# Four graph layers on one core: attention's gathered rows in a ring of three buffers, its first blocks gathered under the counting stage

## The reference

```python
def _L0_gnn_ref(h, edge_index, w, fc_w, fc_b, bias):        # attention, 4 heads
    ...
    e = a_src[:, src] + a_dst[:, dst] + fc_b[0]
    e = jax.nn.leaky_relu(e, negative_slope=0.2)
    seg_max = jax.ops.segment_max(e.T, src, num_segments=n)
    e = jnp.exp(e - seg_max.T[:, src])
    ...
    agg = jax.vmap(lambda m: jax.ops.segment_sum(m, src, num_segments=n))(msg)

def spline_conv(x, row, col, basis, idx, W, b):             # layer 3, 125 kernels
    ...
    gathered = z[col[:, None] * K + idx]
    msg = jnp.einsum('es,eso->eo', basis, gathered)
    out = jax.ops.segment_sum(msg, row, num_segments=N)
    return out / jnp.maximum(deg, 1.0)[:, None] + b

h = jax.nn.elu(spline_conv(ones, row, col, basis, idx, stn1_w, stn1_b))
h = jax.nn.elu(spline_conv(h, row, col, basis, idx, stn2_w, stn2_b))
```

## Time and profile before

| | us |
|---|---|
| median of 3 runs (lowest, highest) | 6663.62 (6661.44, 6674.17) |
| the profiled execution, its time | 6661.12 |
| its span | 6659.3 |
| PE busy | 4881.0 |
| DVE busy | 4480.9 |
| POOL busy | 4088.7 |
| ACT busy | 1826.4 |

### The profile page before, as it was taken

The page is one execution under the profiler, slowest core; times in us unless marked ns, Lnnn a source line. Parts: engine busy times, 40 slices in busy tenths (PEclk is TensorE's granted clock), DMA queues, the critical chain, the costliest instruction groups (busy, mean ns, idle before and its releaser), DMA issues. The chain is left out here.

```text
span 6659.3 us, 106073 instructions
## 1 busy us (share of the span) xinstructions
PE 4881.0 (73%) x34619; PEld 3665.0 (55%) x34619; DVE 4480.9 (67%) x11674; ACT 1826.4 (27%) x3144; POOL 4088.7 (61%) x4097
## 2 busy tenths in 40 slices
PE   5444444676638888888884667999999488888885
PEld 4444444455526666666662434555555366666664
DVE  7555555469957777777771315777776687877775
ACT  1222221458824444444440000000000133333332
POOL 1777777210047777777754254777775577767773
PEclk9999999989969989999996788999999799999997
DMA  4222221123332222222226582111111211111110
GB/s 73 79 78 78 78 78 55 24 57 158 160 85 57 56 56 56 55 55 56 56 47 208 201 262 70 38 37 37 37 37 32 28 21 19 20 19 20 19 20 13
DMA packets 389292, 438.88 MB, mean 66 GB/s; under 512 B 245539, under 2 KB 313104, under 8 KB 388765
## 3 DMA queue, kind: packets, MB, share of 16 engines
q1 hardware_dynamic: 202041, 289.96, 13.9%
q0 software_dynamic: 130592, 126.27, 11.2%
q10 hardware_dynamic: 56528, 21.19, 1.6%
HBM read 355.32 MB, written 82.34 MB: 66 GB/s over the span
## 5 line engine op out<-in xcount | busy, mean ns | idle before, releaser
L967 POOL DMA_INDIRECT at_far<-att_table,at_rec x1184 | 1198.7, 1012 | 759.1 <-DMA at_rec<-rec_r 398.6
L1680 POOL DMA_INDIRECT p_far<-table,p_rec x962 | 964.6, 1003 | 455.5 <-issue 284.9
L2487 PE MATMUL g_l_ps_sum<-g_l_row,g_l_of 128*128 128x392 f32 x3224 | 1063.4, 493 | 19.4 <-DVE g_l_of L2438 19.4
L2409 POOL DMA_INDIRECT g_l_got<-table,g_l_index x806 | 811.6, 1007 | 245.5 <-issue 228.1
L550 POOL DMA_INDIRECT rec_r<-so_r_rec,so_r_place x806 | 788.1, 978 | 245.5 <-issue 245.2
L2487 PEld LDWEIGHTS g_l_ps_sum<-g_l_row,g_l_of 128*128 128x128 f32 x3224 | 614.2, 191 | 469.2 <-DVE g_l_of L2438 20.5
L505 PE MATMUL so_r_look<-so_r_table,so_r_lo_t 128*128 128x26 f32 x1612 | 425.0, 434 | 313.1 <-DVE so_r_table L447 313.1
L2421 DVE TENSOR_SCALAR g_l_row<-g_l_iota,edge_row 128x784 f32<-128x784 f32 x806 | 500.6, 694 | 224.1 <-PE g_l_ps_sum L2487 223.9
L1398 DVE TENSOR_TENSOR p_spread<-at_far,p_mask 128x256 f32<-128x256 f32 x1184 | 444.3, 422 | 299.0 <-PE at_bank L1457 290.8
L1512 ACT COPY p_outer<-at_bank 125x512 f32<-125x512 f32 x1184 | 584.4, 779 | 62.8 <-PE at_bank L1457 62.8
L505 PEld LDWEIGHTS so_r_look<-so_r_table,so_r_lo_t 128*128 128x128 f32 x1612 | 417.5, 356 | 319.6 <-DVE so_r_table L447 165.0
(11 more groups left out here) (492 smaller groups left out, 6679.0 us busy)
## 6 DMA issues: line engine op xcount, KB each, us to landing
adjacent<-ad_by_chunk SPq DMA_DIRECT2D x74, 800.0 KB, 3.3
so_r_row<-pad_src SPq DMA_DIRECT2D x62, 832.0 KB, 6.1
g_l_counts<-adjacent SPq DMA_DIRECT2D x60, 800.0 KB, 7.0
g_l1d_counts<-adjacent SPq DMA_DIRECT2D x59, 800.0 KB, 7.2
so_r_low<-pad_lo_src SPq DMA_DIRECT2D x62, 416.0 KB, 4.5
at_far<-att_table,at_rec POOLq DMA_INDIRECT x1184
p_far<-table,p_rec POOLq DMA_INDIRECT x962
rec_r<-so_r_rec,so_r_place POOLq DMA_INDIRECT x806
```

The source lines that it names most:

```text
L967: pool.indirect_dma_start(out=far[b][:, t, :], out_offset=None, in_=g.att_table[:, :], in_offset=bass.IndirectOffsetOnAxis(ap=rec[b][:, t, ...
L1680: pool.indirect_dma_start(out=sl.far[b][:, t, :], out_offset=None, in_=table[:, :], in_offset=bass.IndirectOffsetOnAxis(ap=sl.rec[b][:, t, ...
L2409: pool.indirect_dma_start(out=got[b][:, j, :], out_offset=None, in_=table[:, :], in_offset=bass.IndirectOffsetOnAxis(ap=index[b][:, j:j + ...
L2487: last = nc.tensor.matmul(ps_sum[k][:], of4[b][:, j, :, :].rearrange("p k f -> p (k f)"), row1[b][:, j, k * COLS:(k + 1) * COLS], start=Fa ...
```

## The change

Three things are moved or changed.

- A class `AttentionRows` holds the record and row buffers of attention, now three of each, and lives around both the counting stage and attention. In attention the loops of all engines hold six blocks, with the first six and the last one outside; POOL's loop holds three gathers.
- `stage_adjacency` gets it: SP loads the records of blocks 0, 1 and 2 ahead of `ad_rec`, and POOL gathers these three blocks (96 indirect DMAs) there instead of in attention.
- For that the node table has to exist before the counts. So the collection of the first spline's sums moves from the counts to `stage_spread`, and `n_p1` and `stage_attention_tables` now run before `stage_adjacency`.

```diff
-def stage_spread(nc, g, name, rows, width, marks, to, scattered=None, by_word=False):
+def stage_spread(nc, g, name, rows, width, marks, to, scattered=None, by_word=False, collect=None):
...
+            elif collect is not None:
+                collected = rows_sem(nc, f"{name}_collected")
+
+                @block.gpsimd
+                def _(pool):
+                    collect_rows(pool, *collect, collected)
...
+class AttentionRows:
+    RING = 3
...
+    def load(self, sp, n, q):
+        sp.dma_start(self.rec[q][:], self.rec_v[:, bass.ds(n * TB, TB), :]).then_inc(self.rec_in[q], 16)
+
+    def gather(self, pool, q, lap):
+        pool.wait_ge(self.rec_in[q], lap * 16 + 16)
+        pool.sem_inc(self.taken, 1)
+        for t in range(TB):
+            pool.indirect_dma_start(out=self.far[q][:, t, :], out_offset=None, in_=self.g.att_table[:, :],
+                                    in_offset=bass.IndirectOffsetOnAxis(ap=self.rec[q][:, t, 0:1], axis=0)).then_inc(self.far_in[q], 16)
...
+        R, far, far_in = ahead.RING, ahead.far, ahead.far_in
+        U = 2 * R
+        loops = o.blocks // U
...
                 for b in two:
-                    load_rec(b, b)
                     load_near(b, b)
                 sl.begin_sync(sp, weights)
...
+                def next_loads(n, u, more_near=True, more_rec=True):
+                    if more_near:
+                        sp.wait_ge(shifts, n + 2)
+                        load_near(n + 2, u % 2)
+                    if more_rec:
+                        sp.wait_ge(sl.positions, n + 2)
+                        ahead.load(sp, n + R, u % R)
...
-                for b in two:
-                    gather(0, b, reused=False)
-                with pool.Fori(1, o.pairs) as i:
-                    for b in two:
-                        gather(i, b)
-                if o.odd:
-                    gather(o.pairs, 0)
+                def gather(lap, q):
+
+                    pool.wait_ge(summed, lap * R + (q - R + 2))
+                    pool.wait_ge(sl.spreads, lap * (R * sl.XS) + ((q - R + 1) * sl.XS + 1))
+                    ahead.gather(pool, q, lap)
+
+                laps = o.blocks // R
+                with pool.Fori(1, laps) as i:
+                    for q in range(R):
+                        gather(i, q)
+                for n in range(laps * R, o.blocks):
+                    gather(n // R, n % R)
...
-                collect_rows(pool, *collect, collected)
+                for q in range(ahead.RING):
+                    ahead.gather(pool, q, 0)
 
             @block.sync
             def _(sp):
+                for q in range(ahead.RING):
+                    ahead.load(sp, q, q)
                 sp.dma_start(rec[:].rearrange("p t w -> p (t w)"), o.rec.rearrange("(p t) w -> p (t w)", p=P)).then_inc(loaded, 16)
...
-    stage_attention_spline(nc, g, ins["L3_gnn_stn2_w"], g.sums_p2)
+    c, _ = scope()
+    with c:
+        ahead = AttentionRows(nc, c, g)
+        stage_adjacency(nc, g, ahead)
+        stage_attention_spline(nc, g, ins["L3_gnn_stn2_w"], g.sums_p2, ahead)
```

More of the change, by code:

```diff
@@ L996, in turn_rows, with one @@
                     last.then_inc(rows_turned, 1)
-                def one(n, b, first=False):
+                def one(n, u, first=False):
+                    b, q = u % 2, u % R
                     pe.wait_ge(terms, n + 1)
@@ L1023, in one @@
                     sl.outer_products(pe, n, third=(copied, n + 2))
-                one(0, 0, first=True)
-                one(1, 1)
-                with pe.Fori(1, o.pairs) as i:
-                    for b in two:
-                        one(i * 2 + b, b)
-                if o.odd:
-                    one(o.blocks - 1, 0)
+                for n in range(U):
+                    one(n, n, first=(n == 0))
+                with pe.Fori(1, loops) as i:
+                    for u in range(U):
+                        one(i * U + u, u)
+                for n in range(loops * U, o.blocks):
+                    one(n, n % U)
                 sl.through_weights(pe, o.blocks - 1)
@@ L1112, in one @@
                         sl.scan(dve, ch, n - 1)
-                    sl.spread(dve, n, b, rest[:2])
+                    sl.spread(dve, n, q, rest[:2])
                     if not first:
                         copy_rows(n - 1, 1 - b, turn + (b - 1))
-                    sl.spread(dve, n, b, rest[2:])
+                    sl.spread(dve, n, q, rest[2:])
                     join(n, b, first)
-                one(0, 0, 0, first=True)
-                one(1, 1, 0)
-                with dve.Fori(1, o.pairs) as i:
+                for n in range(U):
+                    one(n, n, 0, first=(n == 0))
+                with dve.Fori(1, loops) as i:
                     ch.restart()
-                    for b in two:
-                        one(i * 2 + b, b, i)
+                    for u in range(U):
+                        one(i * U + u, u, i)
                 ch.restart()
-                if o.odd:
-                    one(o.blocks - 1, 0, o.pairs)
+                for n in range(loops * U, o.blocks):
+                    one(n, n % U, n // U)
                 sl.scan(dve, ch, o.blocks - 1)
@@ L1148, in store_rows, with one @@
                     sl.load_marks(act, n + 1)
-                def one(n, b, turn, first=False, second=False):
-                    act.wait_ge(far_in[b], turn * (16 * TB) + 16 * TB)
+                def one(n, u, i, first=False, second=False):
+                    b, q = u % 2, u % R
+                    turn, lap = i * R + u // 2, i * 2 + u // R
+                    act.wait_ge(far_in[q], lap * (16 * TB) + 16 * TB)
                     act.wait_ge(turned, n + 1)
-                    nc.scalar.copy(term[:], far[b][:, :, F + 1:F + 5]).then_inc(terms, 1)
+                    nc.scalar.copy(term[:], far[q][:, :, F + 1:F + 5]).then_inc(terms, 1)
                     act.wait_ge(shifts, n + 2)
@@ L1175, in one @@
                     sl.copy_products(act, n)
-                one(0, 0, 0, first=True)
-                one(1, 1, 0, second=True)
-                with act.Fori(1, o.pairs) as i:
-                    for b in two:
-                        one(i * 2 + b, b, i)
-                if o.odd:
-                    one(o.blocks - 1, 0, o.pairs)
+                for n in range(U):
+                    one(n, n, 0, first=(n == 0), second=(n == 1))
+                with act.Fori(1, loops) as i:
+                    for u in range(U):
+                        one(i * U + u, u, i)
+                for n in range(loops * U, o.blocks):
+                    one(n, n % U, n // U)
                 for n in (o.blocks - 2, o.blocks - 1):
```

69 lines of the change are left out of this document (29 added, 40 removed).

## The result

The median of 11 runs went from 6664.8 us (6661.44 to 6674.17) to 6641.94 us (6639.32 to 6664.66): ratio 0.9969, 95% interval 0.996 to 0.9978. The forecast was 6620, range 6610 to 6637. The change makes the kernel faster, by 23 us where 43 were forecast.

A forecast was written before the change was run, and what follows sets the result against it. POOL's gathers, 42.15 us a block, were taken to bound attention. Collection +25.5, counts +2.1, start -24.9 and steady state -45.6 summed to -42.9, 6618.2 us for the profiled execution; the forecast was 6620, range 6610 to 6637.

The forecast's parts named there:

- Collection: Spreading stage: the 25 gathers moved there become its length, 36.9 us instead of 11.38, so +25.5 us.
- Mean and table: Mean, ELU and node table moved ahead of the counts: the same 26.89 us there as behind them, so 0.
- loads and gathers: Counting stage: three record loads cost +2.1 us; the 96 added gathers end inside the stage and cost nothing.
- rival 4: Counting stage: POOL gets nothing done beside DVE, 119.8 us of gathers exposed, net +77, 6741 us; chance 0.02.
- Start: Attention's start: first score 20.7 us after SP's first issue instead of 45.6, p_w's load being next late, so -24.9 us.
- Steady state: Attention's 36 block periods: consumers and POOL end together, 1474 us instead of 1519.6, so -45.6 us.
- Consumers unstarved: Attention: with no late gathers ACT, PE and DVE take 40.9 us a block, 1472.4 us for 36.
- Bodies of six blocks: Attention's loops: six-block bodies cost 0, since the two-block loop's back edge shows no extra time.
- Rival 5: Attention's long loop bodies stall: five back edges and an entry at 2.75 us each, 16.5 more, 6637 us; chance 0.04.
- rival 1: Attention: consumers' own mean stays 41.2 us as clock falls come anyway, net -33.6, 6630 us; chance 0.20.
- POOL's limit: Attention: POOL refilling from block 0's end at 1.317 us a gather allows 1470.6 to 1473 us, first to last score.

The follow-up runs named there:

- e1c_unrolled: Changed kernel with attention's loops of PE, DVE and ACT written out: ratio 0.9955 to the kernel before, first to last score 1482.9 us.
- e9_early_term: Changed kernel, those three loops written out, second spline's weights loaded in the counts, ACT's term copy ahead of its last two product copies: 6610.13 us against 6668.12.
- e7b_best: Changed kernel with attention's PE, DVE and ACT loops written out and the second spline's weights loaded in the counting stage: 6620.76 us against 6668.12, ratio 0.9924.
- e2c_act_dve: Changed kernel with only ACT's and DVE's attention loops written out: ratio 0.9951 to the kernel before, first to last score 1489.1 us.

## Why the prediction was wrong

**Collection, +25.5.** Right: 26.0 in the changed kernel, and 26.3 by the medians when the order was changed alone. The start of 1.55 was 1.9, the pace and the tail as read from the earlier trace rows.

**Mean and table, 0; loads and gathers, +2.1.** Right: 26.9, and 2.2. The 96 gathers took 1.33 us a step beside a DVE that is busy all the time (1517.65 to 1643.70), against 1.25 alone, and DVE's own cycle is 5.20 us beside them and 5.17 behind them. So the full block that the rule of the Trainium skill beside rival 4 describes ("SBUF — State Buffer", "Who interferes with whom") was not seen; whether DVE's operations were in the two-port mode that the rule asks for, no trace shows.

**Start, -24.9.** Right in place and size: -24.4, `p_w` was the next late thing, and with its load moved the first score came 3.2 us after SP's first issue.

**Steady state, -45.6.** This is the step that failed, by 20 us, in "Consumers unstarved: 36 x 40.9 = 1472.4" with its ground "none of the 13 undisturbed blocks was slow". The 40.9 is right for an even block (23 of them, at 40.6 to 41.0). Two costs were left out:

- The back edges. The step "Bodies of six blocks. 0" took the price of a six-block edge from a two-block one. That one costs nothing, as block 7 shows, but its body's code is not loaded again; the body of six is loaded in every block (103 and 60 packets against 10 and 7), and ACT, DVE and PE wait for it at the edge. The cost is 10 to 11 us, four edges of 2.3 to 2.8, and 5.3 in the changed kernel's trace for the clock behind them. Rival 5 had the mechanism and the price (2.75 each) and gave it 0.04; the loop has four back edges, not five, and its entry did not show. By "Instruction fetch mechanics" in the Trainium skill's "Runtime: NRT & Kernel Launch", a taken branch to code that the engine no longer holds makes it fetch before it goes on. The trace agrees: 3 packets of q14 in the 5 us of an edge, and ACT's 1.4 us of idle there are of "issue".
- The clock. In `e1c_unrolled`, with no edges, it costs 15.9 us over 36 even blocks of 40.75, so the mean is 41.2: rival 1's number, and its mechanism, since the clock falls behind PE's idle in the middle of the block. I had read the six blocks of 43.5 in the earlier trace rows as lateness paid twice, because each began after 3.2 us of idle. The undisturbed blocks of before came one or two in a row, and 13 such blocks say nothing of long even runs, in which the written-out kernel loses its clock at every fifth or sixth block.

Rivals 1 and 5 are not exclusive, though the prediction priced them as if they were. Together, with four edges, they give 6630 + 11 = 6641, and 6641.94 was measured; that it fits so closely is partly luck. That the two sit side by side in the changed kernel's own trace is shown; that 11 and 16 make up its 1494.1 (36 x 40.75 = 1467, and 27 more) rests on traces that scatter by 10 us.

**POOL's limit, 1470.6 to 1473.** (Its terms add up to 1470.2.) It was no bound in any run with three buffers. In the changed kernel the last gather starts at 3411.28 and that block's score is made 26 us later, at 3437.56. Even `e9_early_term` leaves it some 7 us (9.8 less the 2.75 of the earlier trace rows).

**What stays open:** what picks the blocks in which the clock stays low for longer. Idle, work and contents of such blocks are those of their neighbours. No run was made that changes the clock alone.

## What to carry to other kernels

The price of a loop edge belongs to the length of the body: take it from a loop as long as the new one, and look at the instruction queues of the DMA view, which tell whether code is loaded in every lap. When a wait is removed, read the price of the clock from blocks that had no wait at all, and from runs of them as long as the new ones will be. Rivals that can happen together must be summed, not only ranked. When a barrier's start is shortened, look at the largest load issued behind it: here 2 MB of weights held 18 us, and moving it cost about 3.

## What the runs showed of the hardware

- Between the two levels of TensorE's clock (1.2 and 2.4 GHz) a stage of even blocks doesn't settle: at equal idle (2.42 us at the start, 4.1 in the middle) blocks of `e1c_unrolled` ran at a mean of 0.96, 0.92 or 0.88 of full speed and took 40.7, 42.1 or 43.6 us. Where the low stretch lay ahead of the middle idle, it cost nothing (40.6 us at 0.92). Taking 0.98 us of idle out of each block (`e9_early_term`) shortened an even block by 0.8 and raised the share of long blocks from a quarter (`e7b_best`) to two thirds; the mean period fell from 41.25 to 40.86, that is by 0.39.
- Bodies of two blocks had 17 packets of code loaded in the stage, bodies of six 163, and the same code written out 136. Only the back edges of the six-block bodies had to be waited for: 2.3 to 2.7 us each in the changed kernel; with PE's loop alone left (`e2c_act_dve`) PE idled 0.7 to 1.2 us longer.
- In two comparisons a block of the same work took about 71.7 us, with 777 us of "issue" in front of one line of matmuls, and all kernels 9500 us on the whole. A change that helps where POOL is the bound was a loss of 0.3 to 0.7% there.
